# Two bias rows of a fused attention/FFN kernel: from TensorE products to adds on GpSimd and VectorE

## The reference

```
h = relu(quant_linear(layernorm(x1), w1, b1))        # stored before the last part as "hidden"
x2 = x1 + quant(h) @ w2q.T * (s_in*s_w) + b2q        # b2q = round(b2 / s) * s,  s = s_in*s_w
x3 = x2 + ln_g * norm(a) + ln_b,  a = norm(x2) @ M + row_m     # attention without softmax, folded to one matrix M per batch
out = x3 + tanh(norm(x3) @ Wc + bias)                # Wc = weight @ aux_weight1 @ aux_weight2
```

## Time and profile before

| | |
|---|---|
| median of 3 runs | 2064.67 us (2063.99 to 2065.43) |
| profiled execution | 2065.53 us, its span 2063.7 us |
| mean granted TensorE clock | 0.978 |
| PE busy over the span | 1937.5 us, 94% |
| DVE busy | 1528.5 us, 74% |
| ACT busy | 1164.4 us, 56% |
| POOL busy | 790.2 us, 38% |

### The profile page before, as it was taken

How to read it: one execution, slowest core, us unless ns; L and a number is a source line. 1 busy time by engine, 2 the same in 40 slices (tenths; PEclk the granted TensorE clock), 3 DMA queues, 4 the chain that set the end, 5 groups by cost and what they waited for, 6 DMA issues and landing times. The chain is left out here.

```text
span 2063.7 us, 30807 instructions
## 1 busy us (share of the span) xinstructions
PE 1937.5 (94%) x9656; PEld 1433.8 (69%) x9656; DVE 1528.5 (74%) x3353; ACT 1164.4 (56%) x3262; POOL 790.2 (38%) x934
## 2 busy tenths in 40 slices
PE   6697799999999999999985999969999999999997
PEld 5576588888887888888862444436777777767775
DVE  6755678888887888887764988867777777777774
ACT  3343677777776777777742333245655555555543
POOL 2201344444444444444430000014555555555553
PEclk9899999999999999999997999999999999999999
DMA  8346211221122212211117999835445445444410
GB/s 269 124 133 214 70 46 58 63 65 53 58 66 77 62 62 67 78 62 42 42 57 287 378 370 352 320 124 195 156 155 180 148 144 171 152 155 155 136 52 37
DMA packets 125253, 280.22 MB, mean 136 GB/s; under 512 B 41120, under 2 KB 51360, under 8 KB 106272
## 3 DMA queue, kind: packets, MB, share of 16 engines
q1 hardware_dynamic: 122256, 276.88, 39.4%
q10 hardware_dynamic: 2832, 1.32, 0.2%
HBM read 168.05 MB, written 110.10 MB: 135 GB/s over the span
## 5 line engine op out<-in xcount | busy, mean ns | idle before, releaser
L1061 POOL TENSOR_TENSOR a_pr<-a_pr,a_rcp 128x512 f32<-128x512 f32 x256 | 266.8, 1042 | 446.1 <-DVE a_rcp L921 446.1
L855 ACT ACTIVATE a_pr<-a_s,a_nmax 128x128 f32<-128x128 f32 x1024 | 361.9, 370 | 55.3 <-DVE a_nmax L914 55.3
L914 DVE TENSOR_REDUCE a_nmax<-a_s 128x4 f32<-128x512 f32 x256 | 176.3, 689 | 96.2 <-PE a_s L60 88.4
L1412 ACT ACTIVATE f_room<-f_X,f_off,f_rs 128x512 f32<-128x512 f32 x128 | 104.5, 816 | 252.5 <-POOL f_off L1683 252.5
L1268 PE MATMUL f_pair<-f_room,w 128*128 128x512 bf16 x1024 | 230.3, 384 | 4.6 <-DVE hmax L1480 3.4
L864 ACT ACTIVATE a_pTh<-a_pt 128x512 fp32r<-128x512 f32 x256 | 153.8, 601 | 137.4 <-PE a_pt L773 137.4
L855 ACT ACTIVATION_READ_ACCUMULATOR a_pr<-a_s,a_nmax 128x1 f32 x1024 | 213.1, 208 | 0.0
L1480 DVE CUSTOM_DVE_ANT_0 f_hf<-f_pair,nb,sh 128x512 f32<-128x512 f32 x256 | 180.7, 749 | 35.5 <-PE f_pair L1268 27.2
L1677 POOL TENSOR_TENSOR f_rs<-f_rs,f_half 128x1 f32<-128x1 f32 x128 | 122.2, 954 | 215.1 <-DVE f_rs L1530 215.1
L929 DVE TENSOR_TENSOR a_pTl<-a_pt,a_pTh 128x512 fp32r<-128x512 f32 x256 | 174.9, 683 | 22.9 <-ACT a_pTh L864 22.7
L1268 PEld LDWEIGHTS f_pair<-f_room,w 128*128 128x128 bf16 x1024 | 99.8, 99 | 121.5 <-issue 5.0
(11 more groups left out here) (382 smaller groups left out, 5061.7 us busy)
## 6 DMA issues: line engine op xcount, KB each, us to landing
hidden<-f_hf SPq DMA_DIRECT2D x60, 1024.0 KB, 6.8
f_hf<-hidden SPq DMA_DIRECT2D x60, 1024.0 KB, 5.3
xb<-x SPq DMA_DIRECT2D x16, 1024.0 KB, 5.4
a_xr<-x SPq DMA_DIRECT2D x64, 256.0 KB, 3.5
x<-a_xr SPq DMA_DIRECT2D x64, 256.0 KB, 2.1
f_X<-x SPq DMA_DIRECT2D x64, 256.0 KB, 5.9
out<-f_X SPq DMA_DIRECT2D x64, 256.0 KB, 5.8
f_room<-x SPq DMA_DIRECT2D x15, 1024.0 KB, 9.5
```

What stands on the lines that cost most here:

```text
L855: last = e.activation(pr[:, t, j, :], s_bank[t][:, j * P:j * P + P], ACT.Exp, bias=nmax[kk % 2][:, t, j:j + 1], accum_out=sums[kk % 2][:, ...
L914: e.tensor_reduce(nmax[kk % 2][:, t, :], s_bank[t][:].rearrange("p (j n) -> p j n", j=4), AX, ALU.max, negate=True).then_inc(*e_max)
L1061: e.tensor_tensor(p, p, rcp[kk % 2][:, t, :].unsqueeze(2).to_broadcast([P, 4, KEYS]), ALU.mult).then_inc(*e_pn)
```

## The change

For the second FFN bias, `ffn2` ends with its sixteenth product. The row is scaled once at the start (`row2`, now with s2 multiplied in), and a new GpSimd helper `based(k+1)`, the last call of each step, adds it to the token tile X one step ahead of `ffn_out`, which then waits for `based` (`e_xc`) instead of the load. For the tanh bias, `last_ffn` ends with its last product, and a new VectorE helper `shifted(k-4)` adds the row to the bank, in place, before `ffn_out(k)`. On ScalarE `tanh(k-4)` waits for `shifted` (`e_fb`) and stands behind `norm(k-2)` instead of ahead of it. The tiles `row_2` and `row_f` go, with the four small instructions that filled them. The third bias row (L1325) stays.

```diff
@@ ffn2
                 for f in range(FC):
-                    e.matmul(y_bank[w % 2], hq[g % 2][:, f, cut(t)], w2[:, f, :], start=f == 0, stop=False)
-                e_rlo.wait_ge(e, 1)
-                e.matmul(y_bank[w % 2], pick[:], row_2[:], start=False, stop=True).then_inc(*e_y)
+                    last = e.matmul(y_bank[w % 2], hq[g % 2][:, f, cut(t)], w2[:, f, :], start=f == 0, stop=f == FC - 1)
+                last.then_inc(*e_y)
@@ last_ffn
-                    three(e, f_bank[w % 2], [x[:, k, :] for x in x3T], [x[:, k, :] for x in wc], k == 0, False)
-                e.matmul(f_bank[w % 2], pick[:], row_f[:], start=False, stop=True).then_inc(*e_f)
+                    last = three(e, f_bank[w % 2], [x[:, k, :] for x in x3T], [x[:, k, :] for x in wc], k == 0, k == KC - 1)
+                last.then_inc(*e_f)
@@ scalar: tanh, and its place in the step
-                e_f.wait_ge(e, w)
+                e_fb.wait_ge(e, w)
...
+                norm(k - 2, mv3, rs3, off3, xn3, e_off3, e_t3, e_xn3)
                 tanh(k - 4)
-                norm(k - 2, mv3, rs3, off3, xn3, e_off3, e_t3, e_xn3)
@@ vector: ffn_out, and the new helper
-                e_x[w % RING].wait_ge(e, w // RING)
+                e_xc.wait_ge(e, w)
                 e_u.wait_ge(e, w)
                 e.tensor_tensor(X[w % RING][:], y, X[w % RING][:], ALU.add).then_inc(*e_x2)
+
+            def shifted(w):
+                if not 0 <= w < NT:
+                    return
+                e_f.wait_ge(e, w)
+                e.tensor_tensor(f_bank[w % 2], f_bank[w % 2], rows[:, 2, :], ALU.add).then_inc(*e_fb)
...
                 low(k - 3, t3_bank, x3T, e_t3h, e_t3l)
+                shifted(k - 4)
                 ffn_out(k)
@@ gpsimd
+            def based(w):
+
+                if not 0 <= w < NT:
+                    return
+                if w == 0:
+                    e_r2.wait_ge(e, 0)
+                e_x[w % RING].wait_ge(e, w // RING)
+                e.tensor_tensor(X[w % RING][:], X[w % RING][:], row2, ALU.add).then_inc(*e_xc)
...
                 biased(k)
+                based(k + 1)
```

More of the change, by code:

```diff
@@ L1209, in rest @@
         pick = sb("pick", [P, P], F32R)
-        row_2, row_f, row_m = sb("row_2", [P, D], F32R), sb("row_f", [P, D], F32R), two("row_m", [P, D], F32R)
+        row_m = two("row_m", [P, D], F32R)
         mask, flag, eps = two("mask", [P, TPG, KEYS], U8), two("flag", [P, TPG]), two("eps", [P, TPG])
@@ L1223, in rest @@
         e_top2, e_all2, e_hscale, e_s2 = ev("top2"), ev("all2"), ev("hiddenscale"), ev("s2")
-        e_half, e_pick, e_zero, e_r2, e_rhi, e_rlo = (ev(n) for n in ("half", "pick", "zero", "row2", "rowhi", "rowlo"))
+        e_half, e_pick, e_zero, e_r2 = (ev(n) for n in ("half", "pick", "zero", "row2"))
+        e_xc, e_fb = ev("xc"), ev("fb")
         e_m, e_mh, e_ml, e_mrh, e_mrl = ev("m", 16), ev("mhi"), ev("mlo"), ev("mrowhi"), ev("mrowlo")
@@ L1432, in _ @@
                     e_zero.wait_ge(e, 0)
-                    e_w.wait_ge(e, 5)
-                    row_high(rows[:, 2, :], row_f, e_rhi)
                 if u in (8, 9, 10, 11):
@@ L1440, in _ @@
                     first_relu(t, q)
-                if t == 0:
-                    e_r2.wait_ge(e, 0)
-                    row_high(row2, row_2, e_rhi)
             for k in STEPS:
@@ L1608, in _ @@
                     e.tensor_tensor(b2[:, cut(u - 1)], b2[:, cut(u - 1)], scr["s2"][:, cut(u - 1)], ALU.mult)
-                if u == 9:
-                    e_rhi.wait_ge(e, 0)
-                    row_low(rows[:, 2, :], row_f, e_rlo)
                 if u in (10, 11, 12, 13):
@@ L1626, in _ @@
                     after(e.tensor_scalar(row2, b2[:], col2[:, 3:4], MAGIC, ALU.mult, ALU.add))
-                    e.tensor_scalar(row2, row2, MAGIC, None, ALU.subtract).then_inc(*e_r2)
                     e.tensor_scalar(scr["s2"][:], scr["sw2row"][:], col2[:, 2:3], None, ALU.mult).then_inc(*e_s2)
-                    e_rhi.wait_ge(e, 1)
-                    row_low(row2, row_2, e_rlo)
-            e_s2.wait_ge(e, 0)
+                    e_s2.wait_ge(e, 0)
+                    e.scalar_tensor_tensor(out=row2, in0=row2, scalar=MAGIC, in1=scr["s2"][:], op0=ALU.subtract,
+                                           op1=ALU.mult).then_inc(*e_r2)
             for k in STEPS:
@@ L1658, in _ @@
             e.memset(half[:], -0.5).then_inc(*e_half)
-            for r in (row_2, row_f, row_m[0], row_m[1]):
+            for r in row_m:
                 last = e.memset(f32(r[:]), 0.0)
```

## The result

The changed kernel takes 2097.43 us, median of 4 runs (2096.21 to 2101.9), beside 2064.93 us for the kernel before on the same chip (4 runs). The ratio on record is 1.0165, 95% interval [1.015, 1.018]; the two medians by themselves give 1.0157. The change makes the kernel slower by 1.6%, clear of noise. The profiled execution took 2098.61 us with a span of 2096.8, against 2065.53 and 2063.7.

What follows compares the result with a forecast made beforehand. A ring of waits over VectorE, GpSimd and ScalarE (10.60 us) was taken as the bound, not TensorE. Steps 4 to 61 +34.5, 62 and 63 +0.3, start +1.7, end +0.3: +36.8 us, forecast 2101.5, range 2094 to 2110.

Steps and rivals of the forecast that it cites:

- the start: Steps 1 and 2: the rounding waits 1.04 us for `based` in each, less 0.4 for bias products: +1.7 us.
- the end: After tile 63's last product: `shifted` ahead of tanh costs 0.69 plus 0.08, less two products of 0.23: +0.3 us.
- VectorE's constant step: Steady steps: VectorE's 10.60 us from scaling to scaling sets the pace, also before 1650 us when TensorE waited for nobody.
- a ring of 10.60 us: Steady steps: waits running round VectorE, GpSimd and ScalarE sum to the whole 10.60 us step; TensorE is not in it.
- `shifted`: Steps 4 to 61: the add before the scaling on VectorE is not hidden and costs 0.595 us per step, +34.5 us.
- Rival D: `shifted` costs 0.69 us per step instead of 0.595: 2107 us; dearer add or crowded GpSimd 0.05, milder half within forecast's 0.84.
- `based` and tanh's place: Steady steps: GpSimd add fits with 0.24 us to spare; `result` ends 0.4 us before the rounding; no cost.
- rival A: `result` ends half a microsecond later, the power precedes the rounding at 0.55 us, ring 10.29 us: 2051 us; chance 0.05.
- 1.1 forecast: Steady steps: TensorE stands still about 1.1 us of each 11.2 us step, some 0.7 of it before the transposes.
- rivals B: TensorE is the pace after all, or `shifted` falls into VectorE's idle time; not slower, 2036 us; chance 0.03.
- C: TensorE's idle times lower its mean granted clock below 0.90; at 0.85 its step is 11.8, about 2136 us; chance 0.03.
- GpSimd first: Steps 1 and 2: a GpSimd add already running shuts out VectorE's rounding; no row used showed it; without it 2.1 us less.

Runs made afterwards that it cites:

- experiments 1: The changed kernel with the tanh add moved into VectorE's idle time, and tanh, result and store one step later: 2063.79 us, 0.9995 of the kernel before.
- 5 to 7: Added wait, split flags, against the kernel before; both biases off TensorE (tanh add behind x2's statistics) 2035.41 us, none off 2059.96, only FFN bias off 2046.80.
- Experiment 4: The whole change plus one wait: VectorE's rounding waits for GpSimd's power and offset for x2; 2067.57 us, 1.001 of the kernel before.
- experiment 5: Both biases off TensorE, rounding waits for GpSimd, tanh add behind x2's statistics, flags split: 2035.41 us, 0.9856 of the kernel before.
- experiment 2: Against the kernel before, only the FFN bias moved to GpSimd, tanh bias still a product on TensorE: 2065.12 us, ratio 0.9999.
- experiment 3: Against the kernel before, only the tanh bias moved to VectorE, FFN bias still a product on TensorE: 2098.83 us, ratio 1.0159.

## Why the prediction was right

The direction, the mechanism and the size of a step held. The time came out 4 us lower than forecast and inside the range. The terms for the start and the end were off, and that their error stayed small is partly luck. The difference of the two profiled executions, cut where the forecast cut it:

| stretch | forecast, us | measured, us |
|---|---|---|
| up to the scaling of tile 4 | +1.7 + 0.6 = +2.3 | 1408.60 - 1408.69 = -0.1 |
| tile 4 to 59 | 55 x 0.595 = +32.7 | 615.88 - 583.42 = +32.5 |
| tile 59 to 63 | +1.4 | 41.13 - 39.69 = +1.4 |
| after the scaling of tile 63 | +0.3 | 31.19 - 31.90 = -0.7 |
| sum | +36.8 (with rounding) | +33.1 |

*What bounds the kernel.* VectorE's constant step against TensorE's 10.51 was the right sign, and experiments 1, 2 and 5 to 7 are its proof from both sides: with a ring of 10.60 us TensorE's load doesn't matter, with a looser one it does.

*`shifted`.* Taken from the start-to-start distance of adds that wait for nothing (0.595 us), not from their duration (0.69); the in-place write of a bank overlaps as the others do. Rival D falls.

*`based` and tanh's place.* Both hidden, as worked out; 0.28 us of room where 0.24 was forecast, 0.44 where 0.4 was. So rival A, which needed `result` half a microsecond later, didn't come. Experiment 4 shows that its arithmetic is right: a ring with a power of 0.55 us makes steps of 10.28.

*TensorE and the clock.* It waits twice a step, as said. The weight loads' waits add up to 0.91 + 0.65 = 1.56 us, more than the 1.1 forecast, but they overlap running products. By the steps, with TensorE's own taken from experiment 5, it stands still 11.20 - 10.08 = 1.12 us. The granted clock stays at its higher level in these steps; rivals B and C fall.

*The start: mis-sized.* The collision is there in both steps. VectorE and GpSimd in step 2, against the earlier trace rows:

```profile
1391.25 3.24 DVE L1497 TENSOR_SCALAR f_room<-f_hf 128x2048 bf16<-128x2048 f32 x2
```
```profile
1391.00 1.27 POOL L1690 TENSOR_TENSOR f_X<-f_X,f_room 128x512 f32<-128x512 f32 x1
```

Two roundings take 3.24 us instead of 2.35, as the first waits for the add: 0.89, where I had 1.04, and the same in step 1. This is the order "GpSimd first" for which I had no row: the rule of the Trainium skill, page "SBUF — State Buffer", section "Who interferes with whom", that whichever comes first shuts the other out, is borne out in both orders.

Most of what the first row of the table lacks lies ahead of the changed steps. The scaling of tile 0, before and now:

```profile
1360.49 0.70 DVE L1538 TENSOR_TENSOR f_pair<-f_pair,s 128x512 f32<-128x512 f32 x1 [0.97 <-PE f_pair L1312]
```
```profile
1358.84 0.70 DVE L1533 TENSOR_TENSOR f_pair<-f_pair,s 128x512 f32<-128x512 f32 x1 [2.15 <-PE f_pair L1311]
```

It comes 1.65 us earlier. ScalarE's first instruction of the last part already starts 1350.68 instead of 1352.08 us, 1.4 us earlier, and VectorE's first copy of the part before the FFN (L984) is at 501.6 instead of 503.0, in code that didn't change; runs of one kernel differ by as much. From the scaling of tile 0 to that of tile 4 the time goes from 48.20 to 49.76 us, +1.56 where the terms say +2.3. Scaling by scaling it is +1.02, +0.11, +0.87 and -0.44, and that isn't what I added up. The first 1.02 is a collision for which I had no term: the new add holds up a 128x4 operation on VectorE, L1554 (rows in the last section). The distance goes from 7.31 to 8.33 us; it is 8.34 in experiment 2 and 7.30 in experiment 3, which has no add on GpSimd. The rounding of step 1 shows only as 0.11, because there `normed` runs 9.21 us after the scaling of tile 1 instead of 10.00. The one of step 2 shows in full. And the sixteen products of tile 4's FFN (L1310 before, L1311 now) took 5.10 us instead of 5.92:

```profile
1394.19 5.92 PE L1310 MATMUL f_pair<-w,f_room 128*128 128x512 bf16 x16 [3.28 <-DVE f_room L1502]
```
```profile
1394.54 5.10 PE L1311 MATMUL f_pair<-w,f_room 128*128 128x512 bf16 x16 [5.03 <-DVE f_room L1497]
```

More of them ran at the full clock: from 1394 to 1400 us 0.70 was granted, where it was 0.59. Why it rose earlier isn't shown.

*The end: mis-sized.* The add at the end of the last tile costs as reckoned: it holds tanh for 0.73 us (2091.32 to 2092.05), where I had 0.77, and from the last product of the last tile's attention to the end of the span it is +0.28. But that attention runs faster. Of its thirteen products the last started 2045.26 - 2041.04 = 4.22 us after the first, partly at half clock:

```profile
2041.04 0.80 PE L58 MATMUL f_pair<-f_m1h,f_x2Th 128*128 128x512 f32 x1 [2.58 <-DVE f_x2Tl L1509]
...
2045.26 0.39 PE L1325 MATMUL f_pair<-f_row_m,f_pick 128*128 128x512 f32 x1
```

Now, with the tile before in the first line:

```profile
2064.56 0.80 PE L58 MATMUL f_pair<-f_m1h,f_x2Th 128*128 128x512 f32 x1 [3.40 <-DVE f_x2Tl L1504]
...
2075.23 0.50 PE L58 MATMUL f_pair<-f_m1h,f_x2Th 128*128 128x512 f32 x1 [1.27 <-DVE f_x2Tl L1504]
...
2078.08 0.39 PE L1325 MATMUL f_pair<-f_row_m,f_pick 128*128 128x512 f32 x1
```

That is 2.85 us, 1.37 less. The half-speed stretch now falls on the tile before, from 2064.56 us to the last of its thirteen products at 2069.84, where the ring covers most of it: the last tile's attention starts 2075.23 - 2065.61 = 9.62 us after its scaling instead of 9.24. Together that is 0.28 - 1.37 + 0.38 = -0.7. I had no term for where such stretches fall.

## What to carry to other kernels

When one engine is 94% busy and another has a step only 1% longer, compare the steps, not the shares: here work moved off the busy one gained nothing, and a 0.6 us instruction put inside the ring of waits cost its full start-to-start time in every step. The same instruction 4 us further on in the same engine's list was free. Before taking work off the engine that looks full, shorten the ring. Here that took two things: an added wait, which lets a short operation of the critical chain run ahead of a long one that shuts it out, and a place in idle time for what that wait crowded, the tanh add and the flags. The wait alone won back only what the change had lost (experiment 4); with both, each product taken off TensorE paid.

## What the runs showed of the hardware

A 128x1 power on GpSimd takes 1.45 to 1.49 us when a float32-to-bfloat16 rounding of 128x2048 on VectorE has started just before it, and 0.55 when the rounding waits for it or none is left, in every step from tile 4 on. The other way round, a rounding that comes 0.25 us after a 1.27 us GpSimd add finishes 0.89 us late. Small VectorE operations are held as well: early in the last part a 128x4 operation with both inputs in SBUF started just after the new add and took 1.18 us instead of 0.16. Before, now, and the new add:

```profile
1367.12 0.16 DVE L1553 SCALAR_TENSOR_TENSOR f_eps<-f_flag 128x4 f32<-128x4 f32 x1
```
```profile
1365.46 1.18 DVE L1554 SCALAR_TENSOR_TENSOR f_eps<-f_flag 128x4 f32<-128x4 f32 x1
```
```profile
1365.35 1.27 POOL L1690 TENSOR_TENSOR f_X<-f_X,f_room 128x512 f32<-128x512 f32 x1
```

TensorE stayed at its higher clock (1.00 granted) through 55 steps with two waits each, of 1.0 and 0.7 us at most. At the end of the kernel before it had stood still for 2.58 us when it waited for a low part, and the products from 2041.63 to 2043.77 us started 0.43 us apart instead of 0.23, which is half clock. In the changed kernel it had stood still for 3.40 us, and those from 2065.15 to 2069.84 us did so. After 1.27 us one tile later they ran at full clock.
